# Keys turned by DMA and normalised by GpSimd, earlier routing of the last groups, and the next expert's number read early

## The reference

```python
x = x + L0_xattn(layernorm(x), ctx_1024, ctx_1024, ...)     # autocorrelation attention
x = x + L0_ffn(layernorm(x), w1, b1, w2, b2)                # ternary weights, gelu
x = x + L1_xattn(ctx_1024, layernorm(x), ...)               # 16 heads of 64; queries from x
x = x + L1_ffn(x, Wg, bg, W1, b1, W2, b2)                   # 8 experts, the top 2 of each row

# L1_xattn: per sequence 64 queries and 128 keys (64 context rows and 64 rows of x)
kv_in = concat([layer_norm(ctx, g1, b1), layer_norm(x, g2, b2)], axis=1)
w = softmax(heads(q) * scale @ heads(k) * scale);  out = (w @ heads(v)) @ Wo
```

## Time and profile before

| | |
|---|---|
| median of 3 runs (lowest, highest) | 1629.28 us (1626.33, 1632.08) |
| the profiled execution, its own time | 1624.12 us |
| its span, first to last instruction | 1622.3 us |
| busy in the span: TensorE matmuls | 1390.7 us (86%) |
| VectorE, ScalarE, GpSimd | 1318.4 (81%), 1283.3 (79%), 1074.1 (66%) |
| mean granted clock of TensorE | 0.944 of full speed |

### The profile page before, as it was taken

How to read it: one execution, slowest core, us unless ns; L and a number is a source line. 1 busy time by engine, 2 the same in 40 slices (tenths; PEclk the granted TensorE clock), 3 DMA queues, 4 the chain that set the end, 5 groups by cost and what they waited for, 6 DMA issues and landing times. The chain is left out here.

```text
span 1622.3 us, 52403 instructions
## 1 busy us (share of the span) xinstructions
PE 1390.7 (86%) x16800; PEld 1179.2 (73%) x16800; DVE 1318.4 (81%) x3902; ACT 1283.3 (79%) x3936; POOL 1074.1 (66%) x1524
## 2 busy tenths in 40 slices
PE   4798899965999999999999999999998188888860
PEld 3677777744888888888888888888886077676750
DVE  3689999885998999999999999999996256565657
ACT  2388888874999999999999999999996166565535
POOL 2478877654666788778877887788875545554550
PEclk9899999997999999999999999999999589999975
DMA  4455544200000000000000000000000134332309
GB/s 151 143 183 210 183 156 185 93 3 25 14 13 12 16 22 25 19 18 20 23 18 18 20 23 20 18 18 23 16 11 18 33 73 77 71 74 61 69 27 311
DMA packets 138950, 101.79 MB, mean 63 GB/s; under 512 B 72184, under 2 KB 119835, under 8 KB 138800
## 3 DMA queue, kind: packets, MB, share of 16 engines
q1 hardware_dynamic: 119200, 78.52, 16.0%
q0 software_dynamic: 8640, 16.93, 3.5%
q10 hardware_dynamic: 10960, 4.46, 1.0%
HBM read 30.09 MB, written 57.16 MB: 54 GB/s over the span
## 5 line engine op out<-in xcount | busy, mean ns | idle before, releaser
L1316 ACT ACTIVATE c_p<-bank,c_nmax 128x128 f32<-128x128 f32 x1024 | 368.9, 401 | 1.9 <-DVE c_nmax L1170 1.2
L1105 POOL TENSOR_TENSOR c_p<-c_p,c_rden 128x512 f32<-128x512 f32 x256 | 266.8, 1042 | 110.1 <-DVE c_rden L1180 105.7
L1316 ACT ACTIVATION_READ_ACCUMULATOR c_p<-bank,c_nmax 128x1 f32 x1024 | 244.1, 241 | 0.0
L1501 POOL DMA_INDIRECT moe_outputs<-e_y,e_to x142 | 146.3, 1031 | 140.3 <-DVE e_y L1527 105.9
L1563 ACT ACTIVATE e_h<-bank,moe_b 128x256 f32<-128x256 f32 x284 | 117.9, 468 | 103.5 <-remote 65.2
L112 PE MATMUL bank<-c_kvT,qk_fused 128*128 128x128 f16 x1024 | 186.0, 220 | 10.8 <-ACT c_kvT L1295 10.4
L1170 DVE TENSOR_REDUCE c_nmax<-bank 128x4 f32<-128x512 f32 x256 | 173.6, 678 | 17.4 <-PE bank L114 14.2
L113 PE MATMUL bank<-c_kvT,qk_fused 128*128 128x128 f16 x1024 | 185.8, 220 | 0.0
L114 PE MATMUL bank<-c_kvT,qk_fused 128*128 128x128 f16 x1024 | 185.8, 220 | 0.0
L1386 PE MATMUL bank<-const,c_p 128*128 128x128 f32 x1024 | 156.0, 275 | 3.2 <-DVE c_pT0rest L1191 1.7
L1148 POOL DMA_INDIRECT moe_slots<-r_rows,r_pos x128 | 131.8, 1030 | 34.8 <-issue 34.8
(11 more groups left out here) (331 smaller groups left out, 5880.5 us busy)
## 6 DMA issues: line engine op xcount, KB each, us to landing
moe_slots<-slot_fill SPq DMA_DIRECT2D x66, 520.0 KB, 5.6
f_z<-moe_outputs SPq DMA_DIRECT2D x32, 256.0 KB, 5.0
...
c_rows<-in_ctx SPq DMA_DIRECT2D x128, 32.0 KB, 2.0
c_rows<-x SPq DMA_DIRECT2D x128, 32.0 KB, 1.8
...
```

The lines of the kernel that those rows point to most:

```text
L1105: pool.tensor_tensor(pr[r % 4][:], pr[r % 4][:], rep(rden[r % 4][:], 2, P), ALU.mult).then_inc(m["pn"], 1)
L1316: last = act.activation(pr[r % 4][:, h, :], SB[r % 2][:, P * h:P * h + P], ACT.Exp, bias=nmax[r % 4][:, h:h + 1], accum_out=den[r % 4][:, ...
L1501: pool.indirect_dma_start(s.z, bass.IndirectOffsetOnAxis(ap=to[t % YBUF][:, h:h + 1], axis=0), ys[t % YBUF][:, h, :], None, bounds_check=2 ...
```

## The change

**Keys by DMA.** The four TensorE transposes and ScalarE's copy go. SyncE issues one transposing DMA a tile from the f16 parts to `c_kvT`, both in SBUF, as soon as GpSimd has written the parts; `c_kvT` has four buffers where it had two. The rows of two tiles are loaded by four DMAs, where it was four for each tile.

**Keys' rows on GpSimd.** The two operations of line 1212 move from VectorE to GpSimd, each with mean and reciprocal deviation as scalars by partition, with two more drains. The statistics have two buffers `c_bn`.

**Tail.** The routing numbers are smaller, and the last three groups (13, 14, 15) have own, still smaller ones, and buffers of their own for rows and positions, so they wait for no earlier group's scatters. The walk ends 17 steps earlier, and its written-out end begins one pass earlier.

**Expert number.** TensorE reads the next tile's expert in the middle of this tile's first products.

The numbers, the helpers and SyncE's program:

```diff
-        AT_STATS, AT_RSTD, AT_KVN, AT_KV, AT_KVT, AT_G, AT_S, AT_PN, AT_PT, AT_O, AT_W, AT_X3 = 15, 13, 12, 11, 7, 6, 3, 2, 0, -1, -5, -9
-        ROUTE_STATS = 14
-        ROUTE_RSTD, ROUTE_XN, ROUTE_XT, ROUTE_LOGITS, ROUTE_TOP, ROUTE_INDEX, ROUTE_MASK = 27, 32, 34, 38, 39, 42, 43
-        ROUTE_HIGH, ROUTE_LOW, ROUTE_STEP, ROUTE_BASE, ROUTE_POS = 44, 47, 45, 46, 47
+        AT_STATS, AT_RSTD, AT_KVN, AT_KV, AT_G, AT_S, AT_PN, AT_PT, AT_O, AT_W, AT_X3 = 15, 13, 12, 11, 6, 3, 2, 0, -1, -5, -9
+        EVEN = GROUPS - 3
+        ROUTE_STATS = 10
+        ROUTE_RSTD, ROUTE_XN, ROUTE_XT, ROUTE_LOGITS = (23, 23, 23), (28, 28, 24), (30, 29, 25), (34, 30, 26)
+        ROUTE_TOP, ROUTE_INDEX, ROUTE_MASK = (35, 31, 27), (38, 32, 28), (39, 32, 28)
+        ROUTE_HIGH, ROUTE_LOW, ROUTE_STEP = (40, 29, 25), (43, 30, 26), (41, 33, 29)
+        ROUTE_BASE, ROUTE_POS = (42, 33, 29), (43, 34, 30)
         AT_KV_LOW = AT_KV - 1
-        ROUTE_SCATTER = (48, 50, 51, 52, 54, 55, 56, 58)
-        FIRST, LO, HI, LAST = -15, 64, 240, CHUNKS + 43
+        ROUTE_SCATTER = tuple(zip((44, 46, 47, 48, 50, 51, 52, 54), (39, 40, 42, 43, 44, 46, 47, 48), (33, 34, 35, 36, 38, 39, 40, 41)))
...
         def group(i, k, at):
 
-            if (k - at) % 16:
+            if known(i):
+                for g in range(GROUPS):
+                    if 16 * i + k == 16 * g + at[min(max(g - EVEN + 1, 0), 2)]:
+                        return g
                 return None
-            g = i + (k - at) // 16
-            return None if known(i) and not 0 <= g < GROUPS else g
+            return None if (k - at[0]) % 16 else i + (k - at[0]) // 16
+
+        def own(g):
+
+            return max(g - EVEN + 1, 0) if known(g) else 0
...
         @block.sync
         def _(sp):
-            def step(i, k):
-                t = 4 * i + k
-                if not (known(i) and i == 0):
-                    sp.wait_ge(m["kvn"], t - 3)
+            def load(n):
+                if n >= 2:
+                    sp.wait_ge(m["kvn"], 2 * n - 2)
                 for half in range(2):
                     rows = slice(64 * half, 64 * half + 64)
-                    sp.dma_start(cs[k][rows, 1 - half, :], cvw[1 - half, t, :, :]).then_inc(c_loaded[k], 16)
-                    sp.dma_start(cs[k][rows, half, :], s.xg(i)[rows, k, :]).then_inc(c_loaded[k], 16)
-            walk(sp, 0, TILES, 4, 4, TILES, step)
+                    to = cs[n % 2]
+                    sp.dma_start(to[rows, :, 1 - half, :], cvw[1 - half, 2 * n:2 * n + 2, :, :].rearrange("t s d -> s t d")).then_inc(c_loaded[n % 2], 16)
+                    sp.dma_start(to[rows, :, half, :], s.xg(n // 2)[rows, 2 * (n % 2):2 * (n % 2) + 2, :]).then_inc(c_loaded[n % 2], 16)
+
+            def turn_keys(v):
+                sp.wait_ge(m["kv"], v + 1)
+                if v >= 4:
+                    sp.wait_ge(m["s"], 4 * (v - 3))
+                sp.dma_start_transpose(kvt[v % 4][:].rearrange("p n a c -> p (n a c)").rearrange("p (b c) -> p b c", b=4),
+                                       kvs[v % 4][:].rearrange("p n b d -> p (n b d)")).then_inc(kvt_in[v % 4], 16)
+
+            load(0)
+            load(1)
+            for v in range(TILES):
+                turn_keys(v)
```

GpSimd's and VectorE's share, then what goes from ScalarE and TensorE:

```diff
-                    pool.tensor_tensor(b[:], b[:], s.mhalf[:, 0:2], ALU.pow).then_inc(m["rstd"], 1)
+                    pool.tensor_tensor(b[:], b[:], s.mhalf[:, 0:2], ALU.pow)
+                if t := tile(i, k, AT_KVN):
+                    v, r, _ = t
+                    pool.drain()
+                    for n in range(2):
+                        last = pool.tensor_scalar(kv[r][:, n, :], cs[r // 2][:, r % 2, n, :], mv[r % 2][:, n, 0:1], rst[r % 2][:, n:n + 1],
+                                                  ALU.subtract, ALU.mult)
+                    last.then_inc(m["kvn"], 1)
                 if t := tile(i, k, AT_KV):
                     v, r, _ = t
-                    pool.wait_ge(m["kvn"], v + 1)
...
-                if t := tile(i, k, AT_KVN):
-                    v, r, g = t
-                    a, b = mv[r % 2], rst[r % 2]
-                    dve.wait_ge(m["rstd"], v + 1)
-                    wait(dve, m["kv"], v - 3)
-                    for n in range(2):
-                        last = dve.tensor_scalar(kv[r][:, n, :], cs[r][:, n, :], a[:, n, 0:1], b[:, n:n + 1], ALU.subtract, ALU.mult)
-                    last.then_inc(m["kvn"], 1)
                 if t := tile(i, k, -ROUTE_STATS):
...
                 if (g := group(i, k, ROUTE_STEP)) is not None:
-                    wait(dve, scattered, 128 * g)
-                    dve.tensor_scalar(dest, dest, float(2 * GT), None, ALU.add)
-                    dve.tensor_copy(first_choice, ix[:, :, 0:1])
+                    q = own(g)
+                    if q:
+                        dve.tensor_scalar(dest[q], s.dst_rows[:, 0:GT].unsqueeze(2), float(2 * GT * g), None, ALU.add)
+                    else:
+                        wait(dve, scattered[0], 128 * g)
+                        dve.tensor_scalar(dest[0], dest[0], float(2 * GT), None, ALU.add)
+                    dve.tensor_copy(first_choice[q], ix[:, :, 0:1])
...
-                    act.activation(kvt[r % 2][:].rearrange("p n a c -> p (n a c)"), KVB[:, 0:512], ACT.Copy).then_inc(m["kvt_copied"], 1)
...
-                if t := tile(i, k, AT_KVT):
-                    v, r, _ = t
-                    pe.wait_ge(m["kv"], v + 1)
...
-                        pe.wait_ge(mr["xt_copied"], g + 1)
-                    for part in range(2):
-                        for b in range(2):
-                            at = 2 * P * part + P * b
-                            last = pe.transpose(KVB[:, at:at + P], kvs[r][:, part, b, :], s.ident_h[:])
-                    last.then_inc(m["kvt"], 1)
```

The expert's number:

```diff
         def _(pe):
+            def of_tile(t):
+                return pe.value_load(tab[0:1, 0, t:t + 1], min_val=0, max_val=EXPERTS - 1)
+
             def first(t, e):
                 pe.wait_ge(x_in[t % XBUF], 16 * (t // XBUF + 1))
                 x = [xt[t % XBUF][:, part, :] for part in range(2)]
                 for b in range(KB):
+                    if b == 2:
+                        ahead = of_tile(t + 1) if t + 1 < NTILE else None
                     if KB * t + b >= 6:
                         pe.wait_ge(m["gelu"], KB * t + b - 5)
                     parts_product(pe, bank(t, b)[:, 0:TSLOT], [weight(part, e, b) for part in range(2)], x).then_inc(m["h"], 1)
+                return ahead
...
-            of = [None, None]
+            of = [None, None, of_tile(0)]
             for t in range(NTILE + 2):
-                now = pe.value_load(tab[0:1, 0, t:t + 1], min_val=0, max_val=EXPERTS - 1) if t < NTILE else None
-                if t < NTILE:
-                    first(t, now)
+                ahead = first(t, of[2]) if t < NTILE else None
                 if t >= 2:
                     second(t - 2, of[0])
-                of = [of[1], now]
+                of = [of[1], of[2], ahead]
```

More of the change, by code:

```diff
@@ L992, in cross_attention @@
     sem = s.sem
-    c_loaded = [sem(f"c_ctx_loaded{n}") for n in range(4)]
-    names = ("stats rstd kvn kv kvt kvt_copied g g_high g_copied s max exp rden pn pt pt_high pt_copied o o_high o_copied w x3")
+    c_loaded = [sem(f"c_ctx_loaded{n}") for n in range(2)]
+    kvt_in = [sem(f"c_kvt_in{n}") for n in range(4)]
+    names = ("stats rstd kvn kv g g_high g_copied s max exp rden pn pt pt_high pt_copied o o_high o_copied w x3")
     m = {n: sem("c_" + n) for n in names.split()}
@@ L997, in cross_attention @@
     mr = {n: sem("r_" + n) for n in route_names.split()}
-    scattered = sem("r_scattered")
+    scattered = [sem(f"r_scattered{n}") for n in range(4)]
     CHUNKS = 4 * TILES
@@ L1002, in cross_attention @@
         parts = lambda name, shape: [sb(name + part, shape, F16) for part in ("high", "rest")]
-        cs = [sb(f"c_rows{n}", [P, 2, D]) for n in range(4)]
+        cs = [sb(f"c_rows{n}", [P, 2, 2, D]) for n in range(2)]
         kv = [sb(f"c_kv{n}", [P, 2, D]) for n in range(4)]
         kvs = [sb(f"c_kv_parts{n}", [P, 2, 2, D], F16) for n in range(4)]
-        kvt = [sb(f"c_kvT{n}", [P, 2, 4, 64], F16) for n in range(2)]
+        kvt = [sb(f"c_kvT{n}", [P, 2, 4, 64], F16) for n in range(4)]
         gs = [parts(f"c_g{n}", [P, 2, HEADS1, SEQ]) for n in range(2)]
@@ L1011, in cross_attention @@
         norm_mul, norm_add = sb("c_norm_mul", [P, 2]), sb("c_norm_add", [P, 2])
-        bst = sb("c_bn", [P, 2, 6])
+        bsts = [sb(f"c_bn{n}", [P, 2, 6]) for n in range(2)]
         mv = [sb(f"c_mv{n}", [P, 2, 2]) for n in range(2)]
@@ L1023, in cross_attention @@
         r_nb = sb("r_shift", [P, GT])
-        rows = sb("r_rows", [P, GT, ROW], F16)
+        rows = [sb(f"r_rows{n}", [P, GT, ROW], F16) for n in range(4)]
         lg = sb("r_logits", [P, GT, EXPERTS])
@@ L1033, in cross_attention @@
         pk = sb("r_pick", [P, 2, GT, EXPERTS])
-        pf = sb("r_posf", [P, 2, GT])
```

(18 more changed lines are left out.)

54 lines of the change are left out of this document (23 added, 31 removed).

## The result

The changed kernel takes 1683.08 us (median of 4 runs, 1681.13 to 1684.90), the kernel before 1630.05 on the same chip: ratio 1.0335, interval 1.0305 to 1.0366. It is slower by 53 us, where 1621 was predicted. The profiled execution took 1682.65 us, its span is 1680.8 us, 58.5 longer than before's.

A forecast was written before the change was run, and what follows sets the result against it. TensorE was taken to set the pace, at 53.6 us a group. Loop +10, before routing -3, start +3, tail -12, experts -6 sum to -8 on 1624.1: 1616, as median 1621, range 1594 to 1641.

The forecast's parts named there:

- GpSimd becomes the engine that sets the loop: Cross attention loop: 5.1 us a group moved onto GpSimd exceeds its 4.3 of cover; 54.4 instead of 53.6, +10 us.
- The price of the pair: GpSimd's two normalising operations a tile: 0.50 us each, bounds 0.34 and 0.64, from one-input rows and two fills.
- the "extreme" of 0.73: Highest price for one GpSimd normalising operation, from line 1119's 256 elements with two inputs: 56.3 us a group, loop +35.
- rival C: Line 1142: each normalising operation takes GpSimd 0.73 us, group 56.3, loop +35, total 1646; chance 0.18.
- The drains: Two more GpSimd drains a tile in the cross attention loop, at 0.14 us each from line 1127.
- rival D: Cross attention: keys come late, TensorE waits 0.3 us a tile on `c_kvt_in`, +19 us, 1640; chance 0.08.
- Less work on TensorE and ScalarE: Loop: TensorE sheds 0.9 to 1.0 us a group, 52.9 to 52.0; ScalarE sheds 2.5, to 49.6.
- The lead of the keys: Steady loop: keys' parts ready four chunks, 13.4 us, before use, so a 3 us late transpose stays hidden.
- Start of the stage: Start of cross attention: transposing DMA's latency, GpSimd's slower normalising and SyncE's queue cost +3 us (2 to 5).
- Before the routing joins: Cross attention up to chunk 44: TensorE's 0.22 or ScalarE's 0.62 us a tile saved, some 12 tiles, -3 us (0 to -7).
- Tail: End of cross attention: waits for groups 13's and 14's scatters vanish, -12 us (-8 to -16).
- Experts: Expert stage: early load of the expert number shortens the gap between tiles, -6 us (0 to -10).

The follow-up runs named there:

- the pair alone: Kernel before with only the keys' rows normalised on GpSimd, two statistics buffers; keys by TensorE, tail and expert number as before: ratio 1.0373, 1626.66 us.
- half of it: Kernel before with GpSimd normalising the first half of the keys' rows and VectorE the second, two statistics buffers: ratio 1.018, 1595.96 us.
- none: Changed kernel with VectorE normalising the keys' rows again; keys by DMA, tail and expert number stay: ratio 0.9992, 1566.29 us.
- the unused DMA: Kernel before plus one transposing DMA a tile, scratch to scratch, at the changed kernel's place, keys still by TensorE: ratio 1.0074, 1577.7 us.
- its later twin: Kernel before plus the same scratch transposing DMA, issued only once VectorE has normalised the next tile's rows: ratio 1.0006, 1625.93 us.
- the later issue: Changed kernel with each keys' DMA issued after the next tile's rows are normalised: ratio 1.1357 normalising on GpSimd, 1.0522 on VectorE.
- Keys alone: Kernel before with only keys by DMA and merged loads; VectorE normalises, routing numbers, buffers and expert's load as before: ratio 1.0014, 1571.37 us.

## Why the prediction was wrong

**GpSimd becomes the engine that sets the loop**: right, and shown by the pair alone (1.0373), half of it (1.018) and none (0.9992). The forecast had it at 54.4 us a group; it is 59.5. The +10 us for the loop became +68.8 from the first to the last tile's sum.

**The price of the pair** is the step that failed: "0.234 + 2 x 0.084 + 124 x 0.8 ns = 0.50 us". Constant and scalars were right, the 0.8 ns an element from two fills was not: an arithmetic operation costs 2.5 to 3.4. Measured 0.79 us, 8 x 0.29 = 2.3 us a group more than the forecast, and above the "extreme" of 0.73, which treated a row with two inputs as an upper bound for one with one. The form of rival C was right, slower, with its turning point at 0.57 us; its price was still too low. Even with 0.79 the forecast's sum gives 49.3 + 4 x (1.58 + 0.28) = 56.7 us a group, so the price alone is not the whole miss. The nearest of the prediction's prices was twice VectorE's 0.34, which it reckoned at 55.9 us a group and left out of the sum.

**The drains** were the second mis-sized term: 0.14 us each, from line 1127, where no scatter is near. Ahead of line 1142 the changed kernel has 12.3 / 34 = 0.36 us and ahead of line 1148 14.1 / 34 = 0.41: 4 x 0.49 = 2.0 us a group. By the trace such a drain leaves 0.16 to 0.20 us where no scatter stands just ahead, and mostly 0.39 to 0.44 where a scatter stands ahead of the multiply before it. The row that showed it was in the trace of before, 8.9 / 37 = 0.24 us on average ahead of line 1113 (groups by form, 600 to 1100 us):

```profile
L1113 POOL TENSOR_TENSOR c_rstd<-c_rstd,c_norm_add 128x2 f32<-128x2 f32 x37 | 7.3, 197 | 8.9 <-issue 7.5
```

**The transposing DMA** lengthened another drain from 0.24 to 17.8 / 33 = 0.54 us, 1.2 us a group, which no step of the prediction had (rival D priced late keys, not this). Not all of it is the DMA's: the run of the pair alone, which has no such DMA, is at 10.6 / 34 = 0.31 us there, so 0.3 of the 1.2 came with the pair and 0.9 with the DMA, about what parts the two runs' 58.7 and 59.5. Line 1151's idle time fell by 0.4. Together 54.4 + 2.3 + 2.0 + 1.2 - 0.4 = 59.5, what was measured. That a transposing DMA at this place lengthens this drain is shown by the unused DMA and its later twin; its 0.9 us in the changed kernel are worked out from rows, since the later issue made the keys late there.

**Less work on TensorE and ScalarE**: forecast 0.9 us a group for TensorE as what was at stake, if GpSimd did not bound. With GpSimd relieved the loop took 54.1 to 54.2, not 52.0: the collision's price was larger than the saving.

**The lead of the keys** was misjudged too: forecast "four chunks or 13.4 us" in the steady state, measured 4.1 to 4.6 in the loop of the changed kernel, for a DMA that lands in up to 3.1. The step numbers gave four chunks, but the engines' walks do not stand at the same step. That TensorE did not wait for the keys in the loop was right by about 1 us, and in part luck; the runs with the later issue show the other side of it.

**Start of the stage**: forecast +3, measured 390.55 for 388.05 in the earlier trace rows, +2.5. **Before the routing joins**: forecast -3 at TensorE's 0.22 us a tile. The size by tile was right: from the first to the fifth sum a tile took (477.38 - 427.77) / 4 = 12.40 us for (477.47 - 426.97) / 4 = 12.63. Keys alone kept 2.3 us of it over the first 14 sums (169.3 for 171.6), the changed kernel nothing (172.0), whose routing joins earlier and meets the pair on GpSimd. **Tail**: forecast -12, measured -11.1 and -10.7 in the traces; of it 4 to 6 us show in the time of the kernels that have it with TensorE's keys and VectorE's pair, since the walk ahead of it is 4.9 us longer. **Experts**: forecast -6, measured 0: the gap between tiles was the load, but not what sets the pace.
